# GpSimd takes other steps' products in the first layer, and the table of jobs changes with them

## The chip, the cores and the metric

The kernel runs on one core of one Trainium2 chip. The metric is the time of one execution on the device in microseconds (us). Lower is better. A core has the engines TensorE (PE in the profile; its weight loads are PEld), VectorE (DVE), ScalarE (ACT), GpSimd (POOL) and SyncE (SP), each with a queue of its own that runs in order, and 16 DMA engines. Engines wait for each other by semaphores.

## What is computed

Two layers run one after the other on x of shape 4 x 128 x 128 x 128, in float32. The change touches the first:

```python
t   = windows of 8 x 8 pixels of x, 64 tokens each, 128 channels
tn  = layernorm(t) * ln_g + ln_b
xi, z = split(tn @ W_in + b_in)                   # 256 channels each
xc  = silu(causal conv over 4 taps of xi + conv_b)
dr, Bm, Cm = split(xc @ W_x)                      # 8, 16, 16
delta = softplus(dr @ dt_w + dt_b)
h_t = exp(delta_t * A) * h_(t-1) + (delta_t * xc_t) * B_t     # 256 channels x 16 states
y_t = sum over the 16 states of h_t * C_t, + xc_t * D
out = (y * silu(z)) @ W_out + b_out + x
```

The second layer normalises over channels, takes a 2D Fourier transform, multiplies with 16 filters, mixes channels, transforms back and ends with a two-matrix network with gelu, plus the residual.

## The kernel before, in words

The first layer is 64 blocks (`NM`), each of 8 image rows (1024 tokens). A block's scan has 32 steps (`NSTEP`): for each half q of its tokens (512) the 16 states. Step n is state n % 16 of half n // 16. Channels lie on the partitions, in two halves of 128, and a scan is one VectorE instruction of 128 x 1024 (`scan`, line 922). It needs a decay, exp(delta * A), from ScalarE (`make_decay`, line 737, two instructions) and a drive, delta * xc * B. In even steps (`DSTEPS`) GpSimd multiplies the drive from `du` = delta * xc and a row of B that a DMA has spread over the partitions (`make_drive`, line 1081); the decay is in PSUM. In odd steps (`RSTEPS`) ScalarE scales the transposed `ut` by a column of B (`scale_u`, line 750, four instructions) and TensorE turns the result into PSUM (`turn_drive`, line 599).

The state times C is a product. In the steps of `BY_GPSIMD` GpSimd takes it, with C spread by a DMA (line 1092); in the other nine VectorE does, with C spread by TensorE into bank 0 of the two job banks (`broadcast_c`, line 587; `times_c`, line 933). TensorE adds the products into `y_acc`, three steps behind (`add_state`, line 612). States and products have 4 buffers each, rows of B and of C 4 each, `ub` and the odd decays 2.

All else of a block is jobs: TensorE writes one of the two job banks (512 columns of PSUM each), and another engine takes it. `JOBS` lists them as (half step, name, slot part, bank). Half step h is 2n or 2n + 1 of step n, and a bank's job waits until the one before in that bank is taken, in bank 0 also until VectorE's earlier products are done. A name ends in (channel half,) token half. z and conv are the input projections, for the block ahead ("front"); xp makes B, C and dr; dt the timesteps; bt and ut the transposes of B and `du`; turn brings y back to channels, out is the output projection; mean and var normalise the block after next; fy is the first Fourier transform of the row. `AT` says at which half step the other engines do their part: `take_conv`, `take_z`, `take_ut1` and so on take a bank, `du1` makes `du` of token half 1 (channel halves 0 and 1), `edge` corrects the first three tokens of each window's convolution (`add_edge`, line 1110, needs all four conv jobs taken), `z1` normalises the first layer's output, `less_mean` and `shift1` are parts of that, `yo` takes fy. Entries like `"rows"`, `"x_in"`, `"x1_out"`, `"x_res"` and `"yo_out"` are steps at which SP issues a DMA. Each engine goes through its own order step by step: its parts at half step 2n, then the scan's operands or products of the step, then its parts at 2n + 1. VectorE's scan n comes ahead of half step 2n. ScalarE makes, in an odd step n, the decays of n + 1 and n + 2, and in an even one `ub` of n + 3; SP loads B 8 steps ahead and C 6 steps ahead. The loop over blocks is unrolled.

The order of the engines' work is thus written out by hand in `JOBS`, `AT` and `BY_GPSIMD`; no functions differ between the two kernels.

Of the kernel before, what the change touches and what calls it, by code (L numbers as in the profile page):

```python
# [62 lines left out]
RSTEPS = tuple(n for n in range(NSTEP) if n not in DSTEPS)  # L63
ALLSTEPS = tuple(range(NSTEP))
UB_AT = {}
BY_GPSIMD = (2, 3, 4, 5, 7, 8, 9, 10, 11, 12, 13, 15, 17, 18, 19, 21, 23, 24, 25, 26, 27, 29, 31)
BY_VECTOR = tuple(n for n in ALLSTEPS if n not in BY_GPSIMD)
NB, NCR, NA, ND, NS_UB, NT, NP = 4, 4, 2, 4, 2, 4, 4
B_LOAD, C_LOAD, ADD_BEHIND = 8, 6, 3
# [1 line left out]


JOBS = [
# [8 lines left out]
]  # L82
CONV_GAP = 2
UT_BY_SCALAR = ('ut10', 'ut00')
Z1_BY_VECTOR = ()

AT = {

    "copy_y": (37, 7), "take_rows": (35, 2), "take_conv": (10, 20, 30, 32), "take_z": (3, 1, 21, 18),
    "softplus0": 39, "softplus1": 11, "silu": 34, "take_bt": (57, 15), "square": (44, 53), "deviation": (45, 56),  # L90
# [1 line left out]

# [2 lines left out]

# [1 line left out]

    "x_in": 16, "rows": (18, 0), "rows_landed": (24, 2), "x1_out": 21, "x_res": 19, "yo_out": 31,
}


# [5 lines left out]
def upto(steps, M, n):  # L107

    return M * len(steps) + nth(steps, n + 1)
# [7 lines left out]
def place_of(steps, M, n, ring):  # L117
    return (M * len(steps) + nth(steps, n)) % ring


def before_in(steps, M, n, ring):

    i = M * len(steps) + nth(steps, n) - ring
    return i // len(steps), steps[i % len(steps)]
# [46 lines left out]
def need(eng, sem, value):  # L171

    if isinstance(value, int) and value <= 0:
        return
    eng.wait_ge(sem, value)  # L175
# [232 lines left out]
def layer0(nc, a, wt, rows_dram, x1_dram, y_dram, blocks):  # L408
    with ExitStack() as ctx:
# [86 lines left out]
        def multiplied(eng, M, n):  # L496
            if n in BY_VECTOR:
                need(eng, s["prod_v_done"], upto(BY_VECTOR, M, n))
            else:
                need(eng, s["prod_g_done"], upto(BY_GPSIMD, M, n))  # L500

# [6 lines left out]
        def _(sp):  # L508
# [10 lines left out]
            def load_b(step):  # L519
                M, p, n = step  # L520
                q, st, slot = n // NS, n % NS, place_of(DSTEPS, M, n, NB)
                need(sp, s["drive_d_done"], upto(DSTEPS, *before_in(DSTEPS, M, n, NB)))
                sp.dma_start(b_all[slot][:], rows_dram[2 * p + q, st:st + 1, :].to_broadcast([P, HT])).then_inc(b_ready[slot], 16)

            def load_c(step):
                M, p, n = step
                q, st, slot = n // NS, n % NS, place_of(BY_GPSIMD, M, n, NCR)
                need(sp, s["prod_g_done"], upto(BY_GPSIMD, *before_in(BY_GPSIMD, M, n, NCR)))
                sp.dma_start(c_all[slot][:],
                             rows_dram[2 * p + q, NS + st:NS + st + 1, :].to_broadcast([P, HT])).then_inc(c_ready[slot], 16)  # L530
# [6 lines left out]
            def body(S, p):  # L537
# [3 lines left out]
                for n in range(NSTEP):  # L541
# [26 lines left out]
                    for k in range(NSTEP):  # L568
                        if k in DSTEPS and (k - B_LOAD) % NSTEP == n and S.step(n + B_LOAD, p):
                            load_b(S.step(n + B_LOAD, p))  # L570
                        if k in BY_GPSIMD and (k - C_LOAD) % NSTEP == n and S.step(n + C_LOAD, p):
                            load_c(S.step(n + C_LOAD, p))
# [153 lines left out]
        def _(act):  # L726
# [39 lines left out]
            def take_ut(S, hf, q):  # L766
                misc = full(act, S, f"ut{hf}{q}")
                act.activation(ut[q][:, :, hf * P:(hf + 1) * P], misc[:].rearrange("p (g d) -> p g d", g=4),
                               ACT.Copy).then_inc(take(S, f"ut{hf}{q}"), 1)
# [74 lines left out]
            def others(S, p, h):  # L844
# [9 lines left out]
                for hf in range(2):  # L854
                    if h == AT["take_ut1"][hf] and S.scan and f"ut{hf}1" in UT_BY_SCALAR:
                        take_ut(S, hf, 1)
                    if h == AT["take_ut0"][hf] and S.front and f"ut{hf}0" in UT_BY_SCALAR:
                        take_ut(S, hf, 0)
# [51 lines left out]
        def _(dve):  # L910
# [63 lines left out]
            def take_ut(S, hf, q):  # L974
                misc = full(dve, S, f"ut{hf}{q}")
                dve.tensor_copy(ut[q][:, :, hf * P:(hf + 1) * P],
                                misc[:].rearrange("p (g d) -> p g d", g=4)).then_inc(take(S, f"ut{hf}{q}"), 1)

            def take_dt(S, hf, q):
                M = S.m + 1 if q == 0 else S.m  # L980
                misc = full(dve, S, f"dt{hf}{q}")
                need(dve, s["softplus_done"], M * 8 + 4 * q + 4)
                need(dve, s["decay_d_done"], upto(DSTEPS, M - 1, NS * (q + 1) - 1))
                need(dve, s["decay_r_done"], upto(RSTEPS, M - 1, NS * (q + 1) - 1))
                need(dve, s["du_done"], (M * 2 + q - 1) * 2)
                dve.scalar_tensor_tensor(delta[:, hf, q * HT:(q + 1) * HT], misc[:], 0.0, soft[:, hf, :], ALU.max,
                                         ALU.add).then_inc(take(S, f"dt{hf}{q}"), 1)
# [31 lines left out]
            def others(S, p, h):  # L1019
# [5 lines left out]
                for hf in range(2):  # L1025
                    if h == AT["take_dt1"][hf] and S.scan:
                        take_dt(S, hf, 1)
                    if h == AT["take_dt0"][hf] and S.front:
                        take_dt(S, hf, 0)
                    if h == AT["take_ut1"][hf] and S.scan and f"ut{hf}1" not in UT_BY_SCALAR:  # L1030
                        take_ut(S, hf, 1)
                    if h == AT["take_ut0"][hf] and S.front and f"ut{hf}0" not in UT_BY_SCALAR:
                        take_ut(S, hf, 0)
# [39 lines left out]
        def _(pool):  # L1073
# [11 lines left out]
            def times_c(step):  # L1085
                M, p, n = step
                slot = place_of(BY_GPSIMD, M, n, NCR)
                M0, n0 = before_in(ALLSTEPS, M, n, NP)
# [563 lines left out]
```

## Time and profile before

| | us |
|---|---|
| median of 3 runs | 9151.34 |
| lowest, highest | 9150.13, 9157.04 |
| the profiled execution's own time | 9160.72 |
| its span, first to last instruction | 9158.9 |
| mean granted TensorE clock | 0.979 |

The profile is one execution. Engine rows give busy time; idle time of an engine is put down to what ended it. The timeline gives each instruction, or a run of like ones, with its start, its length and, in brackets, the idle time before it and who ended that. The first layer takes about the first 6600 us of the span.

### The profile page before, as it was taken

Reading aid. Unit: us, or ns where it says so; the run is one execution under the profiler, and the core shown is the slowest. Engines: PE = TensorE matmul, PEld = TensorE weight load, DVE = VectorE, ACT = ScalarE, POOL = GpSimd, SP = SyncE. Lnnn points to the kernel's source line nnn. Section 1 sums busy time; section 2 is a strip of 40 time slices with the busy share of each in tenths; the row PEclk is TensorE's granted clock in tenths of the full one; section 3 lists DMA queues with packets and bytes.
Section 4 is the critical chain, followed back from the end, with each engine's and each line's share of the span. In section 5 each row is a group of like instructions: output and inputs, shape, how many; then the busy total and the mean of one; then the engine's idle time right before and its main releaser. Section 6 shows DMA issues by size and latency. Waiting matters only on the chain. (4 is left out here: it accounts for less than half of the span.)

```text
span 9158.9 us, 157541 instructions
## 1 busy us (share of the span) xinstructions
PE 8504.2 (93%) x52285; PEld 6526.3 (71%) x52285; DVE 8151.9 (89%) x8082; ACT 7618.8 (83%) x13798; POOL 8038.0 (88%) x3673
## 2 busy tenths in 40 slices
PE   6999999999999999999999999999799999999999
PEld 4666666666666666666666666666599999999788
DVE  5999999999999999999999999999799999999766
ACT  5999999999999999999999999999655555555577
POOL 4999999999999999999999999999799999999500
PEclk8999999999999999999999999999899999999999
DMA  3333433333443344343334443334301101011255
GB/s 92 117 122 127 126 122 124 126 122 123 128 125 124 121 128 127 121 126 123 125 122 124 127 124 122 126 125 124 107 31 38 37 33 38 33 38 37 90 187 177
DMA packets 675841, 982.03 MB, mean 107 GB/s; under 512 B 82761, under 2 KB 280402, under 8 KB 670930
## 3 DMA queue, kind: packets, MB, share of 16 engines
q1 hardware_dynamic: 675282, 974.98, 33.8%
q8 instruction: 302, 4.95, 0.2%
q14 instruction: 257, 2.11, 0.1%
HBM read 828.71 MB, written 146.04 MB: 106 GB/s over the span
## 5 line engine op out<-in xcount | busy, mean ns | idle before, releaser
L1092 POOL TENSOR_TENSOR prod<-state,c_all 128x1024 f32<-128x1024 f32 x1472 | 3477.6, 2371 | 224.1 <-DVE state L922 192.3
L922 DVE TENSOR_TENSOR_SCAN state<-decay_r,drive_r 128x1024 f32<-128x1024 f32 x1024 | 2328.9, 2274 | 244.7 <-PE drive_r L599 149.9
L1081 POOL TENSOR_TENSOR drive_d<-du,b_all 128x1024 f32<-128x1024 f32 x1024 | 2421.3, 2367 | 1.3 <-PE y_acc L612 1.2
L922 DVE TENSOR_TENSOR_SCAN state<-decay_d,drive_d 128x1024 f32<-128x1024 f32 x1024 | 2329.8, 2275 | 79.6 <-ACT decay_d L737 79.6
L612 PEld LDWEIGHTS y_acc<-ident,prod 128*128 128x128 f32 x16384 | 1894.1, 143 | 609.5 <-issue 514.1
L612 PE MATMUL y_acc<-ident,prod 128*128 128x128 f32 x16384 | 2199.3, 278 | 20.4 <-POOL prod L1092 6.4
L1369 DVE SCALAR_TENSOR_TENSOR sum_d<-bank_d,filt,sum_d 128x512 f32<-128x512 f32 x2470 | 1654.7, 743 | 119.3 <-PE bank_d L1277 119.3
L750 ACT ACTIVATE ub<-ut,bt 128x256 f32<-128x256 f32 x4096 | 1736.7, 497 | 12.7 <-issue 0.4
L1416 POOL TENSOR_TENSOR sum_p<-sum_p,scaled 128x1024 f32<-128x1024 f32 x650 | 1554.3, 2391 | 80.5 <-ACT scaled L1327 32.9
L1327 ACT ACTIVATE scaled<-bank_p,filt 128x512 f32<-128x512 f32 x1560 | 944.6, 689 | 622.3 <-PE bank_p L1277 616.0
L737 ACT ACTIVATE decay_d<-delta,neg_a 128x504 f32<-128x504 f32 x2048 | 1309.6, 671 | 39.8 <-DVE state L922 35.2
L737 ACT ACTIVATE decay_r<-delta,neg_a 128x504 f32<-128x504 f32 x2048 | 1340.8, 703 | 0.0
L599 PE MATMUL drive_r<-ident,ub 128*128 128x128 f32 x8192 | 1100.4, 279 | 59.5 <-DVE state L922 40.4
L599 PEld LDWEIGHTS drive_r<-ident,ub 128*128 128x128 f32 x8192 | 946.0, 143 | 199.0 <-issue 136.7
L641 PE MATMUL job_bank<-tn,tap_w 128*128 128x512 f32 (+3 forms) x2048 | 941.3, 587 | 0.8 <-ACT zs L779 0.8
L1277 PE MATMUL bank_d<-th_high,x_high 128*128 128x256 f32 x2600 | 779.9, 300 | 6.3 <-DVE sum_d L1369 1.8
L1277 PE MATMUL bank_d<-th_low,x_high 128*128 128x256 f32 x2600 | 734.6, 283 | 0.0
L1277 PE MATMUL bank_d<-th_high,x_low 128*128 128x256 f32 x2600 | 734.5, 283 | 0.0
L933 DVE TENSOR_TENSOR prod<-state,job_bank 128x1024 f32<-128x1024 f32 x576 | 691.5, 1200 | 7.2 <-issue 1.8
L641 PEld LDWEIGHTS job_bank<-tn,tap_w 128*128 128x128 f32 x2048 | 359.9, 191 | 322.1 <-issue 318.2
L1277 PEld LDWEIGHTS bank_d<-th_high,x_high 128*128 128x128 f32 x2600 | 491.6, 189 | 37.3 <-DVE sum_d L1369 20.3
L1277 PEld LDWEIGHTS bank_d<-th_low,x_high 128*128 128x128 f32 x2600 | 491.6, 189 | 17.0 <-issue 15.3
(156 smaller groups left out, 13497.7 us busy)
## 6 DMA issues: line engine op xcount, KB each, us to landing
c_all<-bc_rows SPq DMA_DIRECT2D x1472, 256.0 KB, 3.3
b_all<-bc_rows SPq DMA_DIRECT2D x1024, 256.0 KB, 3.7
ys<-row_spectra SPq DMA_DIRECT2D x130, 256.0 KB, 2.8
column_sums<-tt SPq DMA_DIRECT2D x130, 256.0 KB, 2.2
x_in<-in_x_dram SPq DMA_DIRECT2D x64, 512.0 KB, 4.9
x_res<-in_x_dram SPq DMA_DIRECT2D x64, 512.0 KB, 5.0
x_rows<-x SPq DMA_DIRECT2D x64, 512.0 KB, 5.1
row_spectra<-z SPq DMA_DIRECT2D x64, 512.0 KB, 4.7
```

The costliest lines, as they stand in the source:

```text
L599: mm = pe.matmul(drive_r[:, hf, g * P:(g + 1) * P], ub[place_of(RSTEPS, M, n, NS_UB)][:, g, hf * P:(hf + 1) * P], wt["ident"][:], start=Tr ...
L612: mm = pe.matmul(y_acc[:, g, hf * P:(hf + 1) * P], prod[place_of(ALLSTEPS, M, n, NP)][:, hf, g * P:(g + 1) * P], wt["ident"][:], start=(n ...
L641: mm = pe.matmul(o[:, :, k:WT], wt["tap_w"][:, K - 1 - k, hf * P:(hf + 1) * P], v[:, :, 0:WT - k], start=(k == 0), stop=(k == K - 1), skip ...
L737: last = act.activation(dst[:, hf, :, 1:WT], delta[:, hf, q * HT:(q + 1) * HT].rearrange("p (w t) -> p w t", t=WT)[:, :, 1:WT], ACT.Exp, s ...
L750: last = act.activation(ub[place_of(RSTEPS, M, n, NS_UB)][:, g, :], ut[q][:, g, :], ACT.Copy, scale=bt[q][:, g, st:st + 1])
L922: dve.tensor_tensor_scan(state[place_of(ALLSTEPS, M, n, NT)][:].rearrange("p h t -> p (h t)"), decay[:].rearrange("p h w t -> p (h w t)"), ...
L1081: pool.tensor_tensor(drive_d[place_of(DSTEPS, M, n, ND)][:], du[:, :, q * HT:(q + 1) * HT], b_all[slot][:].unsqueeze(1).to_broadcast([P, 2 ...
L1092: pool.tensor_tensor(prod[place_of(ALLSTEPS, M, n, NP)][:], state[place_of(ALLSTEPS, M, n, NT)][:], c_all[slot][:].unsqueeze(1).to_broadca ...
L1277: mm = pe.matmul(o, x[p][:, part, b, :], th[:, 2 * pair:2 * pair + 2, :].rearrange("p l h -> p (l h)"), start=(b % 2 == 0 and i == 0), sto ...
L1327: act.activation(scaled[n % 2][:, i, out, :].rearrange("p (b h) -> p b h", b=B), bank_p[:, :, i, :], ACT.Copy, scale=filt[p][:, kind, 2 * ...
L1369: dve.scalar_tensor_tensor(acc, src, factor, acc, ALU.mult, ALU.add).then_inc(s["summed_d"], 1)
L1416: pool.tensor_tensor(acc, acc, scaled[n % 2][:, i], ALU.add).then_inc(s["summed_p"], 1)
```

## The change

Nine products stay with VectorE and 23 with GpSimd, but steps 1 and 14 go to GpSimd and steps 2 and 10 to VectorE. The edge's correction goes from half step 27 to 30. The copy of ut11 goes from VectorE to ScalarE. Half steps, and in places banks, of the other jobs and takes change:

```diff
-BY_GPSIMD = (2, 3, 4, 5, 7, 8, 9, 10, 11, 12, 13, 15, 17, 18, 19, 21, 23, 24, 25, 26, 27, 29, 31)
+BY_GPSIMD = (1, 3, 4, 5, 7, 8, 9, 11, 12, 13, 14, 15, 17, 18, 19, 21, 23, 24, 25, 26, 27, 29, 31)
 JOBS = [
-    (0, "z10", "front", 0), (0, "xp1", "scan", 1), (3, "z00", "front", 1), (4, "conv00", "front", 1),
-    (7, "turn10", "back", 0), (9, "dt01", "scan", 1), (10, "dt11", "scan", 0), (13, "turn11", "back", 1),
-    (15, "bt1", "scan", 1), (16, "z11", "front", 0), (16, "conv10", "front", 1), (20, "z01", "front", 0),
-    (22, "ut01", "scan", 1), (23, "ut11", "scan", 0), (24, "conv01", "front", 1), (25, "conv11", "front", 0),
-    (30, "out0", "back", 1), (31, "out1", "back", 0), (34, "xp0", "front", 1), (37, "dt00", "front", 1),
-    (38, "dt10", "front", 0), (41, "mean0", "ahead", 1), (44, "var0", "ahead", 0), (47, "ut00", "front", 0),
-    (48, "turn01", "scan", 0), (49, "mean1", "ahead", 1), (54, "var1", "ahead", 0), (55, "turn00", "scan", 0),
-    (57, "bt0", "front", 0), (57, "ut10", "front", 1), (61, "fy0", "tail", 1), (63, "fy1", "tail", 1),
+    (0, "z10", "front", 0), (0, "xp1", "scan", 1), (3, "z00", "front", 1), (5, "conv00", "front", 1),
+    (9, "turn10", "back", 0), (10, "dt01", "scan", 1), (11, "dt11", "scan", 0), (13, "turn11", "back", 1),
+    (16, "ut01", "scan", 0), (16, "z01", "front", 1), (17, "conv10", "front", 1), (20, "z11", "front", 0),
+    (20, "bt1", "scan", 1), (24, "ut11", "scan", 0), (24, "conv01", "front", 1), (25, "conv11", "front", 0),
+    (28, "out0", "back", 1), (30, "out1", "back", 0), (34, "xp0", "front", 1), (38, "dt10", "front", 0),
+    (38, "dt00", "front", 1), (42, "mean0", "ahead", 1), (44, "var0", "ahead", 0), (48, "ut00", "front", 0),
+    (49, "turn01", "scan", 0), (49, "mean1", "ahead", 1), (52, "var1", "ahead", 0), (54, "turn00", "scan", 0),
+    (55, "ut10", "front", 0), (56, "bt0", "front", 1), (58, "fy0", "tail", 1), (62, "fy1", "tail", 1),
 ]
-UT_BY_SCALAR = ('ut10', 'ut00')
+UT_BY_SCALAR = ('ut10', 'ut00', 'ut11')
 AT = {
-    "copy_y": (37, 7), "take_rows": (35, 2), "take_conv": (10, 20, 30, 32), "take_z": (3, 1, 21, 18),
-    "softplus0": 39, "softplus1": 11, "silu": 34, "take_bt": (57, 15), "square": (44, 53), "deviation": (45, 56),
-    "less_mean": 47, "deviation1": 50, "z1": (7, 15, 17, 22), "yo": (62, 63),
+    "copy_y": (38, 5), "take_rows": (37, 2), "take_conv": (10, 22, 31, 32), "take_z": (4, 1, 17, 22),
+    "softplus0": 39, "softplus1": 11, "silu": 33, "take_bt": (58, 22), "square": (44, 52), "deviation": (45, 54),
+    "less_mean": 62, "deviation1": 42, "z1": (9, 18, 18, 27), "yo": (62, 62),
-    "tn": (48, 56), "low": (36, 2), "take_dt0": (41, 41), "take_dt1": (14, 14), "take_ut0": (49, 60),
-    "take_ut1": (22, 22), "gate0": (57, 52), "gate1": (9, 14), "x1": (32, 33), "stats": (32, 37), "mean_var": 39,
+    "tn": (49, 55), "low": (37, 2), "take_dt0": (41, 40), "take_dt1": (14, 14), "take_ut0": (48, 56),
+    "take_ut1": (18, 25), "gate0": (54, 51), "gate1": (10, 15), "x1": (33, 33), "stats": (33, 34), "mean_var": 38,
-    "du0": (44, 49), "du1": (19, 21), "edge": 27, "shift1": 63,
+    "du0": (47, 50), "du1": (13, 22), "edge": 30, "shift1": 61,
-    "x_in": 16, "rows": (18, 0), "rows_landed": (24, 2), "x1_out": 21, "x_res": 19, "yo_out": 31,
+    "x_in": 2, "rows": (20, 1), "rows_landed": (24, 8), "x1_out": 31, "x_res": 17, "yo_out": 30,
 }
```

## Rows read from the trace of the kernel before

**Rows 1.** The page, first part: busy time, share of the span, instructions.

```profile
PE 8504.2 (93%) x52285; PEld 6526.3 (71%) x52285; DVE 8151.9 (89%) x8082; ACT 7618.8 (83%) x13798; POOL 8038.0 (88%) x3673
```

**Rows 2.** Stretches: length, PE, PEld, DVE, ACT, POOL busy, clock, DMA share, GB/s.

```profile
422.30:524.90 102.60, 94.13 (x551) 66.57 (x549) 93.32 (x75) 95.65 (x178) 96.44 (x46) 0.97 0.38 122
2950.70:3052.20 101.50, 93.95 (x551) 67.83 (x549) 93.22 (x75) 95.28 (x178) 96.56 (x46) 0.97 0.40 124
3052.20:3152.00 99.80, 91.42 (x551) 65.08 (x549) 93.01 (x74) 95.19 (x178) 96.33 (x46) 1.00 0.40 126
2974.70:2978.10 3.40, 3.40 (x16) 2.63 (x15) 2.61 (x3) 0.88 (x2) 3.40 (x2) 0.50 0.17 64
```

**Rows 3.** Waits, 400 to 6400 us: total, times, longest.

```profile
ACT bt L763 <- PE job_bank L664: 223.6, 119, 3.1
POOL prod L1092 <- DVE state L922: 160.0, 234, 2.2
...
PE job_bank L675 <- DVE delta L986: 128.2, 59, 2.5
...
PE job_bank L670 <- issue: 102.5, 60, 2.1
...
POOL xc L1110 <- ACT xc L779: 80.0, 59, 2.3
```

**Rows 4.** Timeline of ScalarE, the block that begins at 3052.18.

```profile
3078.39 0.22 ACT L763 ACTIVATE bt<-job_bank 128x64 f32<-128x64 f32 x1 [1.29 <-PE job_bank L664]
3078.51 0.87 ACT L832 ACTIVATE z<-x,shift,rstd 128x128 f32<-128x128 f32 x2
3079.28 1.69 ACT L750 ACTIVATE ub<-ut,bt 128x256 f32<-128x256 f32 x4
3080.87 0.87 ACT L832 ACTIVATE z<-x,shift,rstd 128x128 f32<-128x128 f32 x2
3081.64 0.67 ACT L779 ACTIVATE zs<-job_bank,z_b 128x512 f32<-128x512 f32 x1
3082.21 1.27 ACT L737 ACTIVATE decay_d<-delta,neg_a 128x504 f32<-128x504 f32 x2
...
3084.64 0.67 ACT L779 ACTIVATE xc<-job_bank,xc_b 128x512 f32<-128x512 f32 x1
...
3088.40 1.27 ACT L737 ACTIVATE decay_d<-delta,neg_a 128x504 f32<-128x504 f32 x2
...
3118.80 1.06 ACT L791 ACTIVATE soft<-soft 128x1024 f32<-128x1024 f32 x1
```

**Rows 5.** Timeline of VectorE, the same block.

```profile
3066.83 0.69 DVE L992 TENSOR_TENSOR gated<-job_bank,zs 128x512 f32<-128x512 f32 x1 [0.53 <-PE job_bank L679]
3067.76 2.29 DVE L922 TENSOR_TENSOR_SCAN state<-decay_r,drive_r 128x1024 f32<-128x1024 f32 x1 [0.23 <-PE drive_r L599]
...
3074.32 1.26 DVE L986 SCALAR_TENSOR_TENSOR delta<-job_bank,soft 128x512 f32<-128x512 f32 x2
...
3099.85 2.29 DVE L922 TENSOR_TENSOR_SCAN state<-decay_r,drive_r 128x1024 f32<-128x1024 f32 x1 [3.02 <-PE drive_r L599]
...
3119.95 1.29 DVE L986 SCALAR_TENSOR_TENSOR delta<-job_bank,soft 128x512 f32<-128x512 f32 x2 [0.16 <-issue]
```

**Rows 6.** Timeline of TensorE, the same block.

```profile
3075.04 1.12 PE L675 MATMUL job_bank<-xc,diag_d 128*128 128x512 f32 x2 [2.16 <-DVE delta L986]
...
3076.53 0.49 PE L587 MATMUL job_bank<-c_rows,pick 48*128 48x512 f32 x1
3076.95 1.09 PE L612 MATMUL y_acc<-ident,prod 128*128 128x128 f32 x8
...
3078.19 1.04 PE L599 MATMUL drive_r<-ident,ub 128*128 128x128 f32 x8
3079.06 1.02 PE L645 MATMUL job_bank<-tn,z_w 128*128 128x512 f32 x2
```

**Rows 7.** The page, part 6, DMA issues: count, size, us to landing.

```profile
b_all<-bc_rows SPq DMA_DIRECT2D x1024, 256.0 KB, 3.7
```

## The prediction

> **What bounds the kernel now.** I read the page's first part, then the first layer block by block. The layer is 64 blocks of 32 scan steps and all five engines are busy for around nine tenths of it [rows 1], so no share of busy time names the limit. The table by stretches does better. One block without a slow TensorE clock takes 99.8 us, and the block before it takes 101.5 us with the same work, the clock being granted at half (1.2 in place of 2.4 GHz) for a stretch around 2974.7 to 2978.1 [rows 2]. By the starts of the scans, of the 63 distances between blocks 23 are of the short kind (99.9 us), 31 of the long one (101.4 to 101.5) and 9 are over 102; the mean is 101.05. In the short block GpSimd is busy 96.3 us, ScalarE 95.2, VectorE 93.0, TensorE 91.4 [rows 2]: each has 3.5 to 8 us of waiting, and what counts is the order.
>
> The waits [rows 3] and the timelines of the short block, which begins at 3052.18, show a loop of two parts. I give times as us into this block.
> - From the first timestep take (VectorE, 22.14) to the next one (67.77), VectorE waits, ScalarE doesn't. The take frees TensorE for the turn (22.86, after 2.16 us idle [rows 6]); TensorE then works without a gap; ScalarE waits 1.29 us for the bt transposes until 26.21 and then works almost without a gap through 36.22 (the decay of step 12) to the end of the softplus at 67.68 [rows 4]. VectorE's take waits for that: it starts 0.09 us later [rows 5].
> - From 67.77 VectorE runs scan behind scan to the next block at 99.86 (3152.0, the end of the short stretch [rows 2]), and again to 22.14, with 0.76 us of waiting in all.
>
> GpSimd is not in this loop. It waits for scans 160 us and 80.0 us for the edge (59 times, 1.36 us each) in the 59 blocks of the window [rows 3].
>
> **The change, part by part.** It issues the same instructions but one: the copy of ut11 goes from VectorE to ScalarE. All else is order. GpSimd keeps 23 products and VectorE 9.
>
> *Products 1 and 14 against 2 and 10.* Early in the block VectorE multiplies behind scan 3 and no longer behind scan 2: scan 3 ends 1.1 us earlier, the sum up to scan 4 is the same. GpSimd takes product 1 in time that it has and its wait for scan 3 (a part of the 160.0 us) goes. Step 10's product comes on VectorE behind scan 11, that of 14 no longer behind scan 15. VectorE has room before scan 15 (it waits 3.02 us there for TensorE [rows 5]) and none after it, so this gives it 1.1 us behind scan 15, which it then loses again to the wait for out0 and out1 (below). The broadcast of C for step 10 costs TensorE 0.42 us (3076.53 to 3076.95 [rows 6]) in its gapless stretch in place of after it.
>
> *Front of the block.* The gate moves behind scan 5, so its 0.53 and the scan's 0.23 us [rows 5] go. TensorE's thirteen pieces between z00 and the drive of step 7 are the same in another order, so that drive is ready at 19.75 and scan 7 starts some 0.2 us earlier than now; the softplus now waits some 0.7 us for dt11, which comes behind the gate, and ends at 21.6, just in time. The take comes at 21.9: **-0.25 us**.
>
> *From the take to decay 12.* Now 22.14 to 36.22. After: turn at 22.6, then 1.49 for the turn, 0.42 broadcast, 0.93 sum, 0.87 drive of step 9, 0.44 for ut01 (four transposes, half of a drive's eight), and z01, full 1.02 us after its start [rows 6]: 27.8. z01 wants the bank that the gate behind product 6 leaves, which is free in time (27.4). ScalarE waits there for some 0.8 us in place of the 1.29 at bt. Then take 0.57, two quarters of z1 1.54, a pair of decays 2.43, ub 1.60, take of conv10 0.57, some 0.15 of waiting for z11, its take 0.57, bt 0.12 [rows 4]: 35.4. That is **-0.8 us** on 36.22, the 0.25 among it.
>
> *From decay 12 to the softplus.* ScalarE has no gap here, so what is put in is paid in full: the copy of ut11, 0.5 us (a take of 128x512 is 0.57 apart from the next [rows 4]), and the last quarter of z1, 0.77, which moves from half step 22 to 27. **+1.25 us**, less 0.04 of waiting for a scan. The take at 67.77 comes at 68.2.
>
> *GpSimd.* du10 is asked for at half step 13, before its input is there: it would wait some 2 us at 20.5. The edge, at half step 30, stands behind product 13 and waits for the take of conv11 at 48.1, so for about 0.1 us in place of a mean 1.36. Its prod 31 ends about 0.5 us later in the block than now; scans need products four steps back and drives far ahead, so nothing waits for it.
>
> *Out0 and out1* now go into banks that ScalarE frees at half steps 31 and 32 (47.9 and 48.4), while TensorE is ready at about 47.7: 0.2 us of TensorE, and out1 makes VectorE's second x1 and scan 17 wait for about 1 us together. Both lie in VectorE's room before 67.77.
>
> *Second half.* bt0's wait goes (the waits for bt are 119, two a block, 1.88 us each [rows 3]). fy0 and fy1 share a bank and are taken at one half step, so ScalarE waits there for the second, about 1.2 us (0.57 take, then a matmul job like z's, 1.02); the decays of the next scan 0 come after it, at 99.2, and scan 0 is at 100.2. Cover of 0.9 us: I cost it at nothing, and up to 1.2 us a block if it is gone. ut00 is taken as soon as it is made: 0.7 us of ScalarE, hidden likewise. The loads on SP's queue (x_in at step 2 in place of 16, x1_out at 31, yo_out at 30, where it waits for both takes) keep over 2 us to the drive or product that reads them, since rows of B and C are loaded up to four uses ahead and land in 3.7 us or less [rows 7]; costed at nothing.
>
> Sum: -0.82 + 1.25 - 0.04 = **+0.4 us** of a short block, and VectorE is gapless behind it; 64 x 0.4 = +26 us. Against it stands what the 9 long distances of over 102 us pay: in the block at 422.3 (102.60 us [rows 2]) a second slow stretch follows TensorE's idling before ut00 (line 670). In the new order that idling (102.5 us in 60 waits, up to 2.1 [rows 3]) is cut to pieces of less than 1 us; 9 x 1.1 = -10 us. That leaves +16 us on the profiled execution's own 9160.7 (span 9158.9 and 1.8 around it), thus 9177. The median of the runs shown is 9.4 us under that execution: **9167**, +0.17%; chains of some twenty terms like these are good to about 0.2 us a block (13 us) at best. A difference within 0.2% (18 us) can't be told from no change.
>
> Bounds: the sum's terms could be wrong by one missed wait, 1.2 us a block at most (the largest that I cost at nothing), so +77 us; or ScalarE's 0.5 and 0.77 could fall into waits, then -0.8 us a block, -51 us. The slow stretches have bounds of their own: if each short distance became long, 23 x 1.63 = +37 us; if none had one, 31 x 1.6 + 9 x 2.8 = -75 us.
>
> The row says: TensorE idles 2.16 us before the turn in each block, and in about half of them half the clock follows, at a price of 1.63 us [rows 2, 6]. The Trainium skill ("TensorE: Matmul & The Clock Gate", section "HAM oscillation — how this bites in real kernels") says that a kernel whose TensorE keeps waiting between bursts falls back to the slow clock each time and pays the change again and again. The trace agrees in half of the blocks; taken at its word, each block would be a long one, which is the slower rival below.
>
> **The rivals.**
> *Faster.* The 1.25 us don't lengthen the chain, because VectorE, relieved of a copy (0.6 us), the gate's waits and the product behind scan 15, brings scans 12 and 14 earlier, and TensorE's gapless stretch, not ScalarE, holds the decays. And where a short block is shorter, fewer blocks get a slow stretch. For it: ScalarE's 223.6 us at bt are the largest wait of the layer [rows 3] and most of it goes. Against it: ScalarE's rows from 26.21 to 67.68 show nearly no gap, so these decays don't wait now. -0.8 us a block: 9151 - 51 = **9100**.
> *Slower.* One mechanism: TensorE still idles over 2 us before the turn, and also over 2 us instead of 1.6 before mean0, since product 20's broadcast waits for the timestep take behind the later softplus; the half clock comes in nearly every block and lands on turn, sum, drive 9, ut01 and z01, all of which now feed ScalarE's chain. It decides from the point where half of the blocks that are short now have it (+18 us). With it in all, 26 + 37 = +63: **9214**; half of them give +26 + 18 = +44. With fy1's wait uncovered as well it would pass 9280, which I leave out of the range.
> *It doesn't do what it says.* The edge's wait goes, but lands on du10: GpSimd's idle time stays 3.5 to 4.5 us a block. I expect this in any case; alone it changes no time.
>
> **How the numbers follow.** Forecast 0.42, and its own range is 9135 to 9195; faster 0.33; slower 0.25. The range reaches to both rivals and some way past them, 9075 to 9230, for what a missed wait or another share of slow stretches costs. Of the forecast's 0.42, 0.24 lie within 0.2%, 0.12 above and 0.06 below: faster 0.33 + 0.06 = 0.39, same 0.24, slower 0.25 + 0.12 = 0.37.
>
> **What would show it.** Right: ScalarE's bt wait near nothing and a new one at z01; decay 12 near 35.4 and the softplus' end near 68.1 in a short block; du's wait for delta of some 2 us and the edge's under 0.3; TensorE's 2.1 us before the turn still there. Wrong: VectorE waiting between 68 and 100; short blocks under 99.3 or over 100.8; SP's loads ending a wait of GpSimd; another share of slow stretches than about half.

## The result, and the profile after

The changed kernel takes 9168.59 us (median of 15 runs, 9163.97 to 9174.4) against 9151.34 for the kernel before in the same rounds: a ratio of 1.0017, 95% interval 1.001 to 1.0024. It is slower by 17 us. That is a little less than the 0.2% I had called the limit of what can be told; with 15 runs of each the interval leaves out 1 all the same. The forecast was 9167.

The page's first part, the same row as [rows 1]:

```profile
PE 8588.4 (94%) x52285; PEld 6519.6 (71%) x52285; DVE 8093.0 (88%) x8018; ACT 7633.6 (83%) x13862; POOL 8031.9 (88%) x3673
```

The 64 copies of ut11 are seen to move (VectorE 8082 to 8018 instructions, ScalarE 13798 to 13862), and nothing else. The stretches answer to [rows 2]: a block with a slow clock, the next one without, and the slow stretch itself.

```profile
2950.90:3052.60 101.70, 95.26 (x550) 67.46 (x549) 92.20 (x73) 95.52 (x179) 96.29 (x46) 0.97 0.40 123
3052.60:3152.80 100.20, 92.62 (x551) 64.96 (x549) 92.17 (x73) 95.44 (x179) 96.36 (x46) 1.00 0.40 125
2974.50:2977.90 3.40, 3.40 (x16) 2.64 (x15) 2.07 (x3) 3.34 (x7) 3.40 (x3) 0.51 0.01 3
```

A short block is 100.2 us now (99.87 before). By the starts of the scans, 21 of the 63 distances are short (100.20), one is 101.00, nearly all the others are 101.77, and the mean is 101.23 (101.05 before). So the layer ends at 6588.7 in place of 6575.9; what follows it took 2578.0 and 2583.0 us, with the same instructions.

The waits from 400 to 6400 us (total, times, longest), answering to [rows 3]:

```profile
DVE state L922 <- ACT decay_r L737: 229.6, 59, 3.9
...
PE job_bank L675 <- DVE delta L986: 126.5, 59, 2.3
...
ACT zs L779 <- PE job_bank L645: 118.9, 118, 2.4
...
POOL du L1099 <- DVE delta L986: 104.9, 59, 2.2
POOL prod L1092 <- DVE state L922: 101.7, 60, 1.8
...
POOL xc L1110 <- ACT xc L779: 84.1, 59, 2.0
```

ScalarE's 223.6 us at bt are gone, and 118.9 us at the z jobs have come. GpSimd's 160.0 us for scans are 101.7, and 104.9 us for `delta` have come. TensorE's wait for the timestep take is where it was, and so is the edge's: 84.1 us against 80.0. TensorE's 102.5 us before ut00 are gone. VectorE's wait for scan 15, 229.6 us in all, is now ended by ScalarE's decay and no longer by TensorE's drive as in [rows 5].

ScalarE's timeline of the short block, which begins at 3052.62, answers to [rows 4]:

```profile
3080.36 0.69 ACT L779 ACTIVATE zs<-job_bank,z_b 128x512 f32<-128x512 f32 x1 [0.77 <-PE job_bank L645]
...
3087.37 0.69 ACT L779 ACTIVATE zs<-job_bank,z_b 128x512 f32<-128x512 f32 x1 [0.19 <-PE job_bank L645]
3087.96 0.21 ACT L763 ACTIVATE bt<-job_bank 128x64 f32<-128x64 f32 x1
3088.06 1.29 ACT L737 ACTIVATE decay_d<-delta,neg_a 128x504 f32<-128x504 f32 x2
...
3092.09 0.58 ACT L768 ACTIVATE ut<-job_bank 128x512 f32<-128x512 f32 x1
3092.66 1.29 ACT L737 ACTIVATE decay_d<-delta,neg_a 128x504 f32<-128x504 f32 x2
...
3102.75 1.28 ACT L795 ACT_TABLE_LOAD   x1
...
3119.58 1.06 ACT L791 ACTIVATE soft<-soft 128x1024 f32<-128x1024 f32 x1
...
3150.44 0.60 ACT L838 ACTIVATE z<-job_bank 128x512 f32<-128x512 f32 x1 [1.46 <-PE job_bank L696]
```

Less the block's start: z01 at 27.74 after 0.77 us of waiting, decay 12 at 35.44, ut11's copy at 39.47, decay 14 at 40.04, the table load of the silu at 50.13, the softplus' end at 68.02. VectorE's rows of the same block, with [rows 5]:

```profile
3074.34 1.26 DVE L986 SCALAR_TENSOR_TENSOR delta<-job_bank,soft 128x512 f32<-128x512 f32 x2
...
3089.15 1.22 DVE L933 TENSOR_TENSOR prod<-state,job_bank 128x1024 f32<-128x1024 f32 x1 [0.29 <-PE job_bank L587]
3090.28 2.28 DVE L922 TENSOR_TENSOR_SCAN state<-decay_d,drive_d 128x1024 f32<-128x1024 f32 x1
...
3120.72 1.29 DVE L986 SCALAR_TENSOR_TENSOR delta<-job_bank,soft 128x512 f32<-128x512 f32 x2 [0.58 <-issue]
```

The takes start at 21.72 and 68.10. Product 10 waits 0.29 us for its broadcast, and scan 12, behind it, ends at 3092.56: 0.1 us before decay 14 starts. From the second take VectorE again has no gap up to the next block at 3152.81.

TensorE's turn, in the slow block and in the short one, with [rows 6]:

```profile
2973.30 1.13 PE L675 MATMUL job_bank<-xc,diag_d 128*128 128x512 f32 x2 [2.14 <-DVE delta L986]
...
2975.67 1.97 PE L612 MATMUL y_acc<-ident,prod 128*128 128x128 f32 x8
...
3075.06 1.12 PE L675 MATMUL job_bank<-xc,diag_d 128*128 128x512 f32 x2 [2.14 <-DVE delta L986]
...
3076.98 1.09 PE L612 MATMUL y_acc<-ident,prod 128*128 128x128 f32 x8
```

The idle time before the turn is 2.14 us in both (2.16 before the change). In the slow block the sum behind it takes 1.97 us and not 1.09. GpSimd, in the same two blocks:

```profile
3001.01 0.42 POOL L1110 TENSOR_TENSOR xc<-xc,edge 128x96 f32<-128x96 f32 x1 [1.93 <-ACT xc L779]
...
3075.08 1.28 POOL L1099 TENSOR_TENSOR du<-delta,xc 128x512 f32<-128x512 f32 x1 [1.76 <-DVE delta L986]
...
3101.21 0.42 POOL L1110 TENSOR_TENSOR xc<-xc,edge 128x96 f32<-128x96 f32 x1 [0.36 <-ACT xc L779]
...
3124.29 2.38 POOL L1092 TENSOR_TENSOR prod<-state,c_all 128x1024 f32<-128x1024 f32 x1 [1.72 <-DVE state L922]
```

The edge waits 0.36 us in the short block and 1.93 in the slow one; GpSimd's idle time moved to `du`, as forecast. In all it is 3.84 us of the short block.

### The profile page after: what moved, and what is told of

The parts are those of the page before. It is cut to its first block and busy times, and to the rows that moved or that the text cites. A ratio compares the mean times of both kernels' runs of the same rounds, so it can differ in the third digit from the quotient of the medians.

```text
span 9166.7 us, 157478 instructions
## 1 busy us (share of the span) xinstructions
PE 8588.4 (94%) x52285; PEld 6519.6 (71%) x52285; DVE 8093.0 (88%) x8018; ACT 7633.6 (83%) x13862; POOL 8031.9 (88%) x3673
## 5 line engine op out<-in xcount | busy, mean ns | idle before, releaser
L1369 DVE SCALAR_TENSOR_TENSOR sum_d<-bank_d,filt,sum_d 128x512 f32<-128x512 f32 x2470 | 1654.6, 743 | 118.9 <-PE bank_d L1277 118.9
```

Of the source, the lines that this page charges most:

```text
L1369: dve.scalar_tensor_tensor(acc, src, factor, acc, ALU.mult, ALU.add).then_inc(s["summed_d"], 1)
```

## The experiments

Times are medians; each ratio is to the kernel before in the same rounds. "Into the block" is time since the block's scan 0 started.

### ScalarE's two additions: ut11's copy and z1's last quarter

The first run, on the kernel after, gives the copy back to VectorE:

```diff
-UT_BY_SCALAR = ('ut10', 'ut00', 'ut11')
+UT_BY_SCALAR = ('ut10', 'ut00')
```

> The kernel after with the copy of ut11 back on VectorE (half step 25). Main theory: the end of the softplus on ScalarE holds VectorE's timestep take, and the copy's 0.58 us are paid in full there. In a short block the softplus ends at 67.45 in place of 68.03 us, VectorE is ready for the take at 67.5 by the profile after (it waits 0.58 there), so the short block goes from 100.20 to about 99.65; VectorE's copy falls into its 3.9 us of waiting before scan 15. 64 x 0.55 = -35 us, and some more if fewer blocks get the slow clock: 9090 to 9135. Rival (TensorE's gapless stretch holds the loop, ScalarE doesn't): no change, 9160 to 9175.

9193.54 us, ratio 1.0044 [1.0027, 1.0061]; short blocks are 100.38. The main theory (short blocks of 99.65) missed, and so did the rival. VectorE's timeline of a short block, which begins at 2251.01:

```profile
2290.88 0.67 DVE L976 COPY ut<-job_bank 128x512 f32<-128x512 f32 x1
2291.46 2.28 DVE L922 TENSOR_TENSOR_SCAN state<-decay_r,drive_r 128x1024 f32<-128x1024 f32 x1
```

and ScalarE's:

```profile
2291.06 1.29 ACT L737 ACTIVATE decay_d<-delta,neg_a 128x504 f32<-128x504 f32 x2 [0.48 <-DVE state L922]
```

Without the copy ScalarE waits 0.48 us for scan 12 instead, and decay 14 starts at 40.05 into the block, as it does with the copy. Up to decay 14 the copy costs ScalarE nothing, since scan 12 (behind product 10) holds that decay anyway. On VectorE it pushes scans 13 and 14 by 0.58 us; in the short blocks the later decays wait for these, and the table load comes at 50.32 in place of 50.13: +0.19 us, 12 us of the layer. The other 13 of the 25 us against the kernel after are that about three blocks in four are long.

The second brings z1's last quarter (and its second) forward:

```diff
-    ... "z1": (9, 18, 18, 27), ...
+    ... "z1": (9, 16, 18, 18), ...
```

> The kernel after with the quarters of z1 at half steps 9, 16, 18, 18 in place of 9, 18, 18, 27: one falls into ScalarE's wait for z01 (0.76 us in a short block, 2.33 in a long one), none stands between decay 12 and the softplus. Main theory: the softplus ends 0.77 earlier, but VectorE is ready only 0.58 earlier, so the short block is about 99.65, as with the ut11 copy: 9090 to 9135. Rival 1 (ScalarE alone): the full 0.77, 99.43. Rival 2 (TensorE holds the loop): no change, 9160 to 9175.

9134.03 us, ratio 0.9977 [0.9968, 0.9987]: faster than both kernels. Short blocks are 99.93 (-0.27; the main theory had 0.55). ScalarE's timeline of a short block, which begins at 2233.12:

```profile
2273.16 1.29 ACT L737 ACTIVATE decay_d<-delta,neg_a 128x504 f32<-128x504 f32 x2
...
2277.54 1.29 ACT L737 ACTIVATE decay_d<-delta,neg_a 128x504 f32<-128x504 f32 x2 [0.25 <-DVE state L922]
...
2282.98 1.28 ACT L795 ACT_TABLE_LOAD   x1
```

The quarter's 0.77 us are out of the way between decays 14 and 16, but decay 16 then waits for scan 14 and starts 0.34 us later than ScalarE alone would let it (the row shows 0.25 idle, since its instructions overlap), and the last `ub` before the table load starts 0.14 us further behind conv's takes. The table load comes at 49.86, 0.27 us earlier. So the quarter costs 0.27 us of a short block and not 0.77. Of the 35 us against the kernel after, 17 are 63 x 0.27; the others are that here every second block is long, where two in three are after the change. Why the blocks fall so was not settled.

Both edits together:

> The kernel after with both: ut11's copy on VectorE and the quarters of z1 at 9, 16, 18, 18. Main theory: two chains end at the timestep take, ScalarE's and, 0.58 us ahead of it, TensorE's gapless stretch to the drive of step 17 with VectorE behind; taking 1.35 us out of ScalarE gives no more than 0.58, the short block is about 99.65, the time within 10 us of the two single edits (9090 to 9135). Rival (ScalarE alone holds): short block 98.85, -86 us or more: 9060 to 9085.

9192.71 us, ratio 1.0043 [1.0027, 1.006], short blocks 100.39: what the first gave, not the sum; both theories missed. With the copy on VectorE, scan 14 sets decay 16 (it waits 0.85 us), and z1's place no longer matters. The same move on the kernel before:

```diff
-    ... "z1": (7, 15, 17, 22), ...
+    ... "z1": (7, 14, 14, 22), ...
```

> The kernel before with the quarters of z1 at half steps 7, 14, 14, 22 in place of 7, 15, 17, 22: two fall into ScalarE's wait for bt (1.29 us short, 2.86 long). Main theory: VectorE waited only 0.16 us for the softplus in the kernel before, TensorE's chain is right behind, so not over 0.2 us a block: 9130 to 9151, no change or just under. Rival (ScalarE alone holds the loop): -1.3 us a block, 9065.

9153.2 us, ratio 0.9998 [0.9988, 1.0008]: nothing. ScalarE's timeline of the short block that begins at 3253.22 shows why:

```profile
3285.40 0.69 ACT L779 ACTIVATE xc<-job_bank,xc_b 128x512 f32<-128x512 f32 x1 [1.02 <-PE job_bank L641]
...
3288.09 0.69 ACT L779 ACTIVATE zs<-job_bank,z_b 128x512 f32<-128x512 f32 x1 [0.41 <-PE job_bank L645]
...
3289.44 1.28 ACT L737 ACTIVATE decay_d<-delta,neg_a 128x504 f32<-128x504 f32 x2
```

The quarters fill the wait at bt, but ScalarE then waits 1.02 us for conv10 and 0.41 for z01, and decay 12 starts at 36.22 into the block, as in [rows 4]. In the kernel before it is TensorE's row of jobs behind the turn that sets decay 12; the wait at bt has no price of its own.

### Waits that were costed at nothing: fy1 and the edge

On the kernel after, fy0 is taken earlier:

```diff
-    ... "yo": (62, 62), ...
+    ... "yo": (60, 62), ...
```

> The kernel after with the take of fy0 at half step 60 in place of 62, so that fy1's bank is free in time. ScalarE's wait for fy1 (1.44 us a block) goes. Main theory: it is covered, since decay 0 is made 0.2 to 0.3 us before scan 0 wants it: no change, 9160 to 9175. Rival: it is not covered (the trace after shows decay 0 ending at 99.94 with scan 0 at 100.20): faster by 0.1 to 0.3 us a block and fewer slow stretches, 9130 to 9155.

9169.22 us, ratio 1.0022 [1.0012, 1.0032]: no change against the kernel after. The wait that it was to remove is still there, though. ScalarE waits 85.0 us for fy1 from 400 to 6400 us (87.1 in the kernel after), and in the short block that begins at 2954.24:

```profile
3052.03 0.60 ACT L838 ACTIVATE z<-job_bank 128x512 f32<-128x512 f32 x1 [1.43 <-PE job_bank L696]
```

The take of fy0, which holds the bank, was thus not what fy1 waited for, and this run can't say what the wait costs. That it is covered rests on the timeline of the kernel after alone: decay 0 starts 0.25 us behind the take of fy1 and is done 0.2 us before scan 0, and VectorE has no gap there. On the kernel before, the edge alone is moved:

```diff
-    ... "edge": 27, ...
+    ... "edge": 30, ...
```

> The kernel before with one number of the change: the edge's correction at half step 30 in place of 27. Main theory: GpSimd is not in the loop that sets a block's time, so taking its wait for conv11 (80 us in 59 blocks, 1.36 each) away gives nothing: 9140 to 9160; the correction then comes behind product 13, near 49.8 in a short block, where ScalarE's SiLU (49.7) waits for it, so up to 0.4 us a block may be lost: not over 9180. Rival (GpSimd's waits are on the path): -1.3 us a block, 9065.

9146.82 us, ratio 0.9999 [0.9989, 1.0009]. The edge's 80.0 us are gone, and GpSimd waits for scans instead, 235.3 us in place of 160.0; blocks are 99.87 and 101.5 us as before:

```profile
POOL prod L1092 <- DVE state L922: 235.3, 339, 2.2
```

### The exchange of products and the table, each without the other

The new `BY_GPSIMD` alone, on the kernel before (the take of ut11 goes behind VectorE's product 10, on which it depends):

```diff
-BY_GPSIMD = (2, 3, 4, 5, 7, 8, 9, 10, 11, 12, 13, 15, ...)
+BY_GPSIMD = (1, 3, 4, 5, 7, 8, 9, 11, 12, 13, 14, 15, ...)
...
-    ... "take_ut1": (22, 22), ...
+    ... "take_ut1": (22, 24), ...
```

> The kernel before with the products of the change alone: GpSimd takes steps 1 and 14, VectorE 2 and 10 (VectorE's copy of ut11 moves to half step 24, behind product 10, since its bank now comes free behind that product). Main theory: the broadcast of C for step 10 (0.42 us) comes into TensorE's gapless stretch, and product 10 (1.1 us) stands between scans 11 and 12, on which ScalarE's single decay buffer waits; this delays scans 12 to 14 and the take: +0.4 to +1.2 us a block, 9175 to 9230. Rival (what the prediction held: VectorE has 3 us of room before scan 15, so only the 0.42 count): 9151 to 9180. Rival 2 (GpSimd's wait for scan 3 mattered): faster than 9140.

9241.63 us, ratio 1.0103 [1.0087, 1.012], over the range of every theory; most blocks are about 102.1. TensorE's timeline of the block that begins at 2776.45:

```profile
2812.16 0.47 PE L587 MATMUL job_bank<-c_rows,pick 48*128 48x512 f32 x1
...
2813.05 1.04 PE L612 MATMUL y_acc<-ident,prod 128*128 128x128 f32 x8
2815.17 0.63 PE L670 MATMUL job_bank<-ident,du 128*128 128x128 f32 x4 [1.08 <-issue]
```

and ScalarE's:

```profile
2822.72 0.69 ACT L779 ACTIVATE xc<-job_bank,xc_b 128x512 f32<-128x512 f32 x1 [1.23 <-PE job_bank L641]
```

C for product 10 now lies in bank 0 just where ut11 wants that bank: TensorE waits 1.08 us in its gapless stretch, ScalarE 1.23 us for conv01, and scan 15 starts at 49.65 into the block instead of 47.67.

The other half, the kernel after with the old products:

```diff
-BY_GPSIMD = (1, 3, 4, 5, 7, 8, 9, 11, 12, 13, 14, 15, ...)
+BY_GPSIMD = (2, 3, 4, 5, 7, 8, 9, 10, 11, 12, 13, 15, ...)
```

> After, with GpSimd's products of steps 2 and 10 as before and the new table of jobs and the edge's new place kept: the exchange of products is taken away alone. Main theory: the three chains end within a few tenths of a microsecond of one another, and the exchange by itself is close to neutral: TensorE's stretch from the last turn is as long as it is now, scan 12 is no longer behind product 10, so that ScalarE's decay 14 starts at 39.9 to 40.1 as in the kernel after, the table load stays at 50.0 to 50.2, and the shortest blocks take 100.0 to 100.4 us; the time is 9150 to 9180 us. Rival: the exchange is what makes the kernel slower, and without it the kernel is where it was before, with shortest blocks of 99.87 and 9140 to 9155 us. Second rival: the new table needs the new products (product 14 on GpSimd frees VectorE when scan 15 ends), and without them the blocks are longer by 0.5 or more, 9190 us or over.

9240.06 us, ratio 1.0098 [1.0081, 1.0115]; two blocks in three are 101.9, the others 103.5. The main theory missed and the second rival was right. TensorE's timeline of the block that begins at 2983.83:

```profile
3035.01 0.49 PE L587 MATMUL job_bank<-c_rows,pick 48*128 48x512 f32 x1
3036.92 0.68 PE L689 MATMUL job_bank<-out_w,gated 128*128 128x128 f32 x4 [1.42 <-issue]
```

VectorE's and ScalarE's:

```profile
3035.60 1.22 DVE L933 TENSOR_TENSOR prod<-state,job_bank 128x1024 f32<-128x1024 f32 x1 [1.85 <-PE job_bank L587]
```

```profile
3046.96 1.02 ACT L815 ACTIVATE y_tok<-y_acc 128x1024 f32<-128x1024 f32 x1 [1.41 <-PE y_acc L612]
```

The table now has out0 at half step 28, ahead of the broadcast for product 14: VectorE's product waits 1.85 us for it, out1 (bank 0) waits until the product is taken, and TensorE is late up to the sum that ScalarE's copy of y needs. The softplus ends at 69.7 into the block, not at 68.0.

### TensorE's idle time before the turn

The sum of step 4 goes ahead of the turn and of the broadcast, into TensorE's idle time, in the kernel after:

```diff
-    ... (13, "turn11", "back", 1),
+    ... (14, "turn11", "back", 1),
...
+                    ahead = n == 7
+                    if ahead and S.step(n - ADD_BEHIND, p):
+                        add_state(S.step(n - ADD_BEHIND, p))
-                    if n - 1 in BY_VECTOR and S.scan:
+                    if not ahead and n - 1 in BY_VECTOR and S.scan:
                         broadcast_c(S, S.step(n - 1, p))
                     jobs(S, p, 2 * n)
-                    if S.step(n - ADD_BEHIND, p):
+                    if ahead and S.scan:
+                        broadcast_c(S, S.step(n - 1, p))
+                    if not ahead and S.step(n - ADD_BEHIND, p):
                         add_state(S.step(n - ADD_BEHIND, p))
```

> The kernel after with TensorE's sum of product 4 pulled ahead of the turn that waits for the timestep take (and the broadcast of C for step 6 behind that turn, as now). TensorE's idle time before the turn goes from 2.14 to 1.2 us, and 0.9 us of work leaves its gapless stretch. Main theory: two gains. The chains behind the take get shorter by 0.76 to 0.93 us (short block 99.3 to 99.5), and without the long idling the clock isn't lowered there, so that there are nearly no blocks of 101.8 any more: mean 99.5 in place of 101.23, 63 x 1.7 = -109, 9060, at least 9040 to 9090. Rival (the slow clock has nothing to do with this idling): two in three blocks still pay 1.57, so -0.85 x 64 = -55, 9110 to 9120. Rival 2 (the loop is held elsewhere): no change of the short block.

9096.91 us, ratio 0.9945 [0.9928, 0.9961]. TensorE's timeline of the block that begins at 2919.15:

```profile
2941.60 1.12 PE L675 MATMUL job_bank<-xc,diag_d 128*128 128x512 f32 x2 [1.27 <-DVE delta L991]
...
2943.51 1.09 PE L599 MATMUL drive_r<-ident,ub 128*128 128x128 f32 x8
2945.00 0.63 PE L670 MATMUL job_bank<-ident,du 128*128 128x128 f32 x4 [0.39 <-issue]
```

The granted clock of the stretch from the turn on, and of one 48 us later, behind another idle time of TensorE (2.10 us, before mean0):

```profile
2941.60:2945.00 3.40, 3.01 (x15) 1.87 (x16) 1.87 (x3) 3.40 (x8) 3.38 (x2) 1.00 0.14 43
2989.70:2993.10 3.40, 3.40 (x17) 3.26 (x16) 3.40 (x3) 3.40 (x8) 2.37 (x2) 0.51 0.03 12
```

The idle time before the turn is 1.27 us, no slow stretch comes there in any block but the first, and all the steady blocks but two take 100.10 us (these two take 100.92, see the last section). The kernel after pays for the slow stretches 41 x (101.77 - 100.20) = 64 us; with 63 x 0.10 that is 70 of the 72 us measured between the two. What I had expected beside, a shorter chain by the sum's 0.9 us, came out at 0.10, so the time is just above the range of 9040 to 9090: ut01 waits for its bank until product 6 is through (the 0.39 us of the last row, and drive 9 stands ahead of it).

With z1 moved as in the second experiment, on top:

> The kernel after with the sum of product 4 ahead of the turn and the quarters of z1 at 9, 16, 18, 18. Alone the first gave blocks of 100.10 us, all alike, and 9097; the second took 0.27 us off a short block (ScalarE's decay 16 then waits for scan 14). Main theory: the two add, since z1's quarter leaves the same stretch and nothing changes the idling before the turn: 99.85 a block, 64 x -0.26 = -17: 9075 to 9085. Rival (the gain of the z1 edit was one of fewer slow blocks alone): 9090 to 9100.

9081.47 us, ratio 0.9922 [0.9905, 0.9938], nearly all blocks 99.83 to 99.85: the 0.27 us again. The same two edits on the kernel before (`turn11` to 14 and the order of the sum; then also `"z1": (7, 14, 14, 22)`):

> The kernel before with TensorE's sum of product 4 pulled ahead of the turn (and the broadcast for step 6 behind the turn, as now). Main theory (the slow clock follows the 2.16 us of idling, here as in the kernel after): idling 1.2 us, nearly all blocks of the short kind, and up to 0.5 us off it, because bt comes earlier: mean 99.4 to 99.9 in place of 101.05, 9047 to 9078; the change's own cost then is 20 to 50 us between this and the same edit in the kernel after (9097). Rival (the other idling places, before mean0 and ut00, then bring slow stretches that cost as much): 9100 to 9150.

9073.74 us, ratio 0.9912 [0.9895, 0.9928]: the fastest of all. The stretch of a short block (99.47 us), TensorE's turn and ScalarE's bt in it:

```profile
2512.10:2611.60 99.50, 91.62 (x551) 65.08 (x549) 93.07 (x75) 95.31 (x178) 96.53 (x46) 1.00 0.39 126
```

```profile
2534.95 1.12 PE L675 MATMUL job_bank<-xc,diag_d 128*128 128x512 f32 x2 [1.29 <-DVE delta L991]
```

```profile
2537.86 0.22 ACT L768 ACTIVATE bt<-job_bank 128x64 f32<-128x64 f32 x1 [0.86 <-PE job_bank L664]
```

TensorE's jobs behind the turn come 0.4 us earlier: the wait at bt is 0.86 us in place of 1.29, decay 12 starts at 35.82 in place of 36.22, and the short block is 99.47 in place of 99.87. Slow stretches behind the idle time before ut00 (2.06 us) remain and cost up to 0.75 us of some blocks; the mean is 99.84. Between this run and the same edit in the kernel after (9096.91) lie 23 us. With the slow stretches at the turn gone from both, the change still costs, 0.63 us of the short block.

> The kernel before with the sum ahead of the turn and the quarters of z1 at 7, 14, 14, 22. The z1 edit alone changed nothing (9153 beside 9154), since TensorE's chain ended 0.16 us ahead of ScalarE's. Main theory: with 0.5 to 0.9 us off TensorE's chain ScalarE holds the take, and the quarter in the bt wait now counts: 0.2 to 0.6 us a block below the edit of the sum alone, 9020 to 9060. Rival (VectorE's scans 12 to 14 hold the decays): within 5 us of the sum's edit alone.

9075.45 us, ratio 0.9914 [0.9897, 0.993]: z1's place gives nothing here; the main theory missed and the rival's figure was right, but not its reason. ScalarE no longer waits at bt and waits 0.63 us for conv10 and 0.41 for z01 instead, and decays 12 and 14 start at 35.83 and 39.99 into the block, as without the edit. TensorE's jobs hold decay 12 here too.

## Why the prediction came out

**The short block: right.** +0.4 us forecast, 0.33 measured (99.87 to 100.20). Its steps, forecast and measured, us into the block:

| step | forecast | measured |
|---|---|---|
| first timestep take | 21.9 | 21.72 |
| z01 on ScalarE, its wait | 27.8, 0.8 | 27.74, 0.77 |
| decay 12 | 35.4 | 35.44 |
| softplus' end, take | 68.1, 68.2 | 68.02, 68.10 |
| next scan 0 | 100.2 | 100.19 |

ScalarE gets to decay 12 0.78 us earlier than in [rows 4]; the copy takes 0.44 of that, z1's last quarter 0.77, and the table load is 0.43 us late. The 0.78 us come from the new order of TensorE's jobs behind the turn. They don't come from the removed wait at bt: the kernel before with that wait filled has decay 12 where it was.

**The price of the two additions: right as a sum of the timeline, wrong as a cause.** "ScalarE has no gap here, so what is put in is paid in full" failed. It holds for the rows as they lie, not for what the additions cost. Given back to VectorE, the copy turned into a wait of 0.48 us for scan 12, which stands behind product 10 and its 0.29 us of waiting, and the quarter, moved away, brought 0.27 us of its 0.77. The faster rival, in which the additions fall into waits, was wrong too: product 10 now stands in the chain of VectorE's scans 12 to 14, and TensorE starts the drive of scan 15 at 47.07 into the block, 0.53 us later than before. How much of the 0.33 us each of these chains would ask for by itself wasn't parted further.

**The slow stretches: the sum right, the words not.** I had -10 us from the blocks over 102. The excess over the short block was 63 x (101.05 - 99.87) = 74 us and is 63 x (101.23 - 100.20) = 65: -9. The blocks over 102 went, all but the first, and TensorE's idle time before ut00 with them. The slower rival, half the clock behind the turn in nearly every block, did not come: 41 of 63 blocks have it, and 38 had it before. I wrote "in about half of them", counting only the 31 (two of which, 100.8 and 100.9, had their slow stretch elsewhere). Its price was 1.63 forecast and is 1.57. The row says that after 2.14 us without work half the clock (0.51 granted) follows in two blocks of three. The Trainium skill ("TensorE: Matmul & The Clock Gate", section "HAM oscillation — how this bites in real kernels") has a loop pay in each round; the waits in its example are of 3 to 5 us, those before the turn here of 2.14. The trace agrees in 41 of 63 blocks, and by that rule all 22 others would be long. That the idle time before the turn brings the slow stretch is shown by filling it: at 1.27 us (1.29 in the kernel before) no block but the first has one there. Why some blocks are spared at 2.14 us stays open.

**GpSimd: right but for the edge.** `du` waits 1.76 us (2 forecast). The edge's wait was to be under 0.3: it is 0.36 in short blocks and 1.9 in long ones, 84.1 us in all and no less than before. I had worked it out for a block with the full clock alone. The run with only the edge moved shows that the wait has no price.

**What was costed at nothing: held, by the timeline.** fy1's 1.46 us and ut00's 0.9 are covered, since VectorE has no gap behind the second take, but no run took them away; no row of after has one of SP's loads ending a long wait.

**The product exchange: right only with its table.** By the two half runs the exchange alone costs +1.03%, the table (with the copy and the edge) alone +0.98%, both together +0.17%. My working took the order as a whole, and so came out right; it did not see that each half has a wait of over a microsecond in bank 0 that the other removes. The exchange, the front of the block and the table weren't parted further.

**From the layer to the median: partly luck.** I had forecast the profiled execution at 9177 and taken off 9.4 us, by which the one before lay over its median. It came at 9168.59, which is the median itself. In these two executions the layer ends 13 us later (16 forecast), what follows it is 5 us shorter, which no term had, and the span is 8 us longer; the medians differ by 17. So the layer's sum was right to 3 us, and the 9167 is so near 9168.59 because two errors of 8 and 9 us cancel. The 9.4 us may lie in the blocks over 102. The run with only the edge moved has the same short and long blocks as the kernel before, but in its profiled execution (9143.80) it has 5 blocks over 102 in place of 9, and the 63 distances are 8 us shorter in all. The number of such blocks thus differs from one execution to another, and with it the worth of my -10.

## What to carry to other kernels

Where three engines' chains end within half a microsecond of each other, an edit's price can't be read from one timeline: what read as 0.44 and 0.77 us gave back nothing and 0.27. Take the edit out once, and see which wait takes its place, and also whether the wait that it was to remove is gone. Who computes a product also decides how long a shared bank is held, so an exchange and the table of the jobs in that bank are one change; either alone was about six times as dear here as both. And a TensorE idle time that seems to cost nothing may be what lowers its clock: one instruction group moved into it brought 0.8%, more than the whole reordering moved either way.

## What the runs showed of the hardware

The same idle time of 2.14 us before the turn, in blocks with the same instructions, is followed by the half clock in some blocks and by the full clock in others: long, long, short after the change, long, short in the run with z1 early. With 1.27 us none but the first block had it there. A slow stretch is not always paid: in the run with the sum ahead the clock still falls in some blocks (0.51 granted) behind TensorE's 2.10 us of idling at 68.8 into the block, where VectorE and not TensorE holds the chain, and these blocks take 100.10 us with it or without. Only where it lasts 6.8 us in place of 3.4 is it paid there: the two blocks of 100.92, and the one of 101.00 in the kernel after.
